# An order of its own for attention's first stage, with Pool's loads moved and routed rows scattered per token, in a two-layer AdaLN network on one core

## The reference, cut to what matters

```python
# x: 2 x 2048 x 256.  Layer 0
h = layernorm(x) * (1 + ca) + sa
Q, K, V = h @ W_q.T, h @ W_k.T, h @ W_v.T          # 16 heads of 16, rotary on Q and K
scores = Qr @ Kr.T / 4, causal;  pattern = softmax(scores)
x = x + ga * (pattern @ V) @ W_o.T
h = layernorm(x) * (1 + cb) + sb
x = x + gb * (h + h @ expert_w[argmax(h @ gate_w.T)].T)
# Layer 1
h = layernorm(x) * (1 + ca) + sa
x = x + ga * toeplitz_block(h)                      # u * T(v), with projections
h = layernorm(x) * (1 + cb) + sb
xn = h * rsqrt(mean(h * h) + eps) * ln_w
vals, idx = top_k(xn @ Wg + bg, 2);  topk_w = softmax(vals)
y_e = (silu(xn @ W1a[e] + b1a[e]) * (xn @ W1b[e] + b1b[e])) @ W2[e] + b2[e]     # F = 1024, 8 experts
x = x + gb * sum over the two chosen e of topk_w[e] * y_e
```

## Time and profile before

| what | value |
|---|---|
| median of 3 runs (lowest to highest) | 2665.64 us (2662.68 to 2666.26) |
| the profiled execution: its time / its span | 2663.03 us / 2661.1 us |
| mean granted clock of TensorE | 0.916 |
| busy: PE / DVE / ACT / Pool | 84% / 64% / 47% / 32% |
| DVE's 640 reduces of maxima (line 892) | 651.9 us, 1061 ns mean |
| Pool's 512 masks (line 705) | 143.3 us, 292 ns mean |
| zero fill of `y_slots` | 73 DMAs of 512 KB |
| first score product to the last of attention | about 301 to 1210 us |

### The profile page before, as it was taken

One profiled execution on the slowest core, in us unless ns is written; L12 is line 12 of the kernel. 1 busy time (PEld: TensorE's weight loads), 2 busy tenths in 40 slices (PEclk: granted clock), 3 DMA queues, 4 the chain that ended last, 5 costly groups with the idle time before them and its releaser, 6 DMA issues. The chain is left out here.

```text
span 2661.1 us, 39725 instructions
## 1 busy us (share of the span) xinstructions
PE 2231.8 (84%) x12968; PEld 1413.0 (53%) x12968; DVE 1693.0 (64%) x2599; ACT 1260.2 (47%) x2419; POOL 859.6 (32%) x1041
## 2 busy tenths in 40 slices
PE   3984898999989899996799699853999999999930
PEld 1762233333333333325577456553888888888830
DVE  4873877777777778844688768753545555545544
ACT  1331376766757677773223344412445555545520
POOL 2445302122121211110655413543223333323256
PEclk8996699999999999998899899966999999999975
DMA  4368604042140400002860100115444344434324
GB/s 164 107 144 166 91 2 65 5 62 35 33 65 3 64 3 3 2 1 67 351 256 0 31 1 17 40 44 182 136 152 141 133 149 141 146 121 133 123 76 126
DMA packets 138336, 238.26 MB, mean 90 GB/s; under 512 B 14768, under 2 KB 101552, under 8 KB 136752
## 3 DMA queue, kind: packets, MB, share of 16 engines
q1 hardware_dynamic: 122128, 181.44, 19.8%
q0 software_dynamic: 14928, 50.35, 10.7%
q10 hardware_dynamic: 1104, 4.20, 1.1%
HBM read 150.88 MB, written 85.07 MB: 89 GB/s over the span
## 5 line engine op out<-in xcount | busy, mean ns | idle before, releaser
L892 DVE TENSOR_REDUCE tile_max<-p_m 128x2 f32<-128x1024 f32 (+3 forms) x640 | 651.9, 1061 | 172.5 <-PE p_m L751 102.8
L854 ACT ACTIVATE probs<-p_s 128x512 f32<-128x512 f32 (+3 forms) x1280 | 596.3, 534 | 273.2 <-PE p_s L764 267.7
L2052 PE MATMUL p_up<-f_xT,f_w 128*128 128x512 f32 (+1 forms) x2304 | 468.9, 352 | 8.6 <-POOL f_w L2182 8.6
L2052 PEld LDWEIGHTS p_up<-f_xT,f_w 128*128 128x128 f32 x2304 | 372.2, 189 | 62.0 <-issue 8.9
L2182 POOL TENSOR_TENSOR f_w<-f_raw,f_w 128x1024 fp32r<-128x1024 f32 x96 | 230.9, 2409 | 504.0 <-ACT f_w L2104 504.0
L751 PE MATMUL p_m<-ka,qa 96*128 96x512 bf16 (+3 forms) x1280 | 363.3, 366 | 27.1 <-PEq L327 15.3
L705 POOL TENSOR_SCALAR_AFFINE_SELECT probs<-probs 128x128 f32<-128x128 f32 x512 | 143.3, 292 | 732.2 <-ACT probs L854 724.7
L764 PE MATMUL p_s<-qa,ka 99*128 99x512 bf16 (+3 forms) x1280 | 353.5, 353 | 11.5 <-ACT probs L854 6.9
L778 PE MATMUL p_o<-probs,va 128*32 128x512 f32 (+3 forms) x2560 | 305.9, 550 | 29.5 <-POOL probs L705 29.5
L2067 PE MATMUL p_y<-f_w,f_hidden 128*128 128x256 f32 x1872 | 261.8, 286 | 23.0 <-DVE f_y L2158 11.7
L2067 PEld LDWEIGHTS p_y<-f_w,f_hidden 128*128 128x128 f32 x1872 | 241.1, 188 | 45.4 <-issue 23.5
(11 more groups left out here) (242 smaller groups left out, 2602.3 us busy)
## 6 DMA issues: line engine op xcount, KB each, us to landing
y_slots<-zeros SPq DMA_DIRECT2D x73, 512.0 KB, 5.6
f_raw<-in_W1a SPq DMA_DIRECT2D x24, 1024.0 KB, 6.5
f_raw<-in_W1b SPq DMA_DIRECT2D x24, 1024.0 KB, 8.6
f_raw<-in_W SPq DMA_DIRECT2D x24, 1024.0 KB, 11.1
qk_scr<-parts SPq DMA_DIRECT2D x48, 256.0 KB, 2.3
qa<-qk_scr POOLq DMA_DIRECT2D x42, 256.0 KB, 15.6
ka<-qk_scr POOLq DMA_DIRECT2D x42, 256.0 KB, 17.4
v_scr<-wqkv_raw SPq DMA_DIRECT2D x32, 256.0 KB, 3.1
```

The lines of the kernel that those rows point to most:

```text
L854: nc.scalar.activation(probs[:, (buf * UNITS + n) % NPROBS, h, lo:CH], p_s[:, s_bank(("exp", HG * n + h), buf), lo:CH], ACT.Exp, scale=DH ...
L892: nc.vector.tensor_reduce(out=tile_max[:, 2 * hp:2 * hp + 2, i, bank], in_=p_m[:, at_bank, :, 0:width], op=ALU.max, axis=AX.X).then_inc(ma ...
L2052: last = nc.tensor.matmul(p_up[:, f % 2, ab, 0:size], w1[:, wh, ab * KT + kt, f * P:(f + 1) * P], xT[:, t % 2, xh, kt, 0:size], start=(kt, ...
```

## The change

1. *Projections*: the ones rows of ka0 are set by Pool right after `rstd`, ahead of the three subtractions. The first stage's loads go in three parts, after chunks 4, 5 and 6 (4, 4 and 5 DMAs), on ACT as before; ACT's loop over the chunks is unrolled.
2. *Attention*: stage 0 has a lead of 24 maxima (chunks 0 and 1) and a table of its own, three maxima a unit in the first 18. The other stages keep their table. The ones rows of ka1 and ka2 are set after unit 11's mask of stage 0, and the loads of stage s + 2 are issued after unit 11's mask of stage s (1 to 5), in place of those of stage s + 3 after the last mask of stage s.
3. *Top-1 experts*: no zeros, no zero fill.
4. *Layer 1*: rows get 258 columns, the last two the token's number and its first expert's number + 1. DVE waits for the routing tables before its first centring, copies the token numbers, and has one small operation more in each of the five choices and one at the end.
5. *Routed experts*: DVE finds for each slot the row of `y_rows` that it belongs to (token number, plus `SECOND` if it is the second choice, an own dump row if it is none), five small operations a tile, and SP waits for them before it loads the next rows. Pool scatters `f_y`, 78 indirect DMAs of 128 rows, a tile's after the last first-layer piece of the tile behind it. SP's 24 stores go.
6. *Combine*: SP loads both rows of all tokens in 16 plain DMAs of 512 KB, ACT does the first product, DVE the other three; Pool has nothing to do.

```diff
                 root(nc, pool, k, 0)
+                pool.wait_ge(k.rstd_ready, 1)
+                nc.gpsimd.memset(k.ka0[QROWS:QROWS + SPLIT, :, :], 1.0).then_inc(ones0_set, 1)
+                pool.wait_ge(ones0_set, 1)
                 for n, cols in enumerate(columns):
...
+                def load_first_stage(third):
+
+                    if third == 0:
+                        for qk in range(2):
+                            act.wait_ge(parts_stored[qk], 16 * SPLIT * CPS)
+                        act.wait_ge(va_stored, 16 * NHG * CPS)
+                    load_scores_rows(act, k, 0, k.qa0, k.ka0, k.stage0_loaded, range(2 * third, 2 * third + 2))
+                    if third == 2:
+                        load_values(act, k, 0, k.va0[:, :, :], k.stage0_loaded)
...
-                    if isinstance(i, int) and i == NCH - 2:
-                        load_first_stage()
                     if not last_chunk(i):
                         round_hT(i + 1, 1 - par)
                     take_v(i)
                     split(i, 0)
                     split(i, 1)
+                    if isinstance(i, int) and CPS <= i < CPS + 3:
+                        load_first_stage(i - CPS)
...
-        MAX_LEAD = 22
+        MAX_LEAD, FIRST_LEAD = 2 * 22, 24
...
+        FIRST_MAXIMA = [(2, 1)] * 18 + [(1, 1)] * 6 + [(2, 1), (1, 1)] * 2 + [(1, 1)] * 12
+        assert sum(map(sum, FIRST_MAXIMA)) == NMAX + MAX_LEAD - FIRST_LEAD
+        FIRST_TURN = {9: (2, False), 20: (3, False), 24: (0, True), 32: (1, True)}
...
-                for rows in ka:
-                    last = nc.gpsimd.memset(rows[QROWS:QROWS + SPLIT, :, :], 1.0)
-                last.then_inc(ones_set, 1)
                 for s in range(NS):
                     for n in diag_no:
                         mask(s, n)
-                    if s + NBUF < NS:
-                        load(s + NBUF)
+                        if diag_no[n] == 2 * TPC - 1:
+                            if s == 0:
+                                pool.wait_ge(diag_masked, 2 * TPC)
+                                for n1 in range(1, NBUF):
+                                    nc.gpsimd.memset(ka[n1][QROWS:QROWS + SPLIT, :, :], 1.0).then_inc(ones_set, 1)
+                                pool.wait_ge(ones_set, NBUF - 1)
+                            elif s + NBUF - 1 < NS:
+                                load(s + NBUF - 1)
 
...
                             pe.wait_ge(max_placed, 16 * (CPS * s + c + 1))
+                            if c == 0 and not first(s):
+                                pe.wait_ge(ones_set, NBUF - 1)
...
-                for u in range(2 * MAX_LEAD):
+                for u in range(FIRST_LEAD):
                     if u >= 2:
                         pe.wait_ge(max_taken, u - 1)
                     maximum(0, 0, u, u % 2)
                     if ends_chunk(u):
                         turn_maxima(max_units[u][0], max_units[u][0])
-                pe.wait_ge(ones_set, 1)
...
-                sp.wait_ge(zeros_set, 1)
-                with sp.Fori(0, NSLOT // ST) as t:
-                    sp.dma_start(k.y_slots[at(t, ST, ST), :].rearrange("(p u) d -> p (u d)", p=P), zeros[:, :]
-                                 ).then_inc(slots_zeroed, 16)
-                sp.wait_ge(slots_zeroed, 16 * (NSLOT // ST))
...
                 c_own.add(nc.vector.memset(cum[:, :, :], 0.0))
+                dve.wait_ge(route_loaded, 16 * ROUTE_LOADS)
+                c_own.add(nc.vector.tensor_copy(row_ids[:, :, 0], token_no))
                 dve.wait_ge(rstd_all, 1)
...
                         sp.wait_ge(turned, t)
+                        sp.wait_ge(y_to_ready, t)
...
-                def store(t):
-                    size = SIZES[t]
-                    row = sp.value_load(k.rows[0:1, t:t + 1], min_val=0, max_val=NSLOT - ST)
-                    sp.wait_ge(y_ready, t + 1)
-                    sp.dma_start(k.y_slots[bass.ds(row, size), :].rearrange("(u p) d -> p u d", p=P), y[:, 0:size // P, :]
-                                 ).then_inc(y_stored, 16)
-
...
+                def find_rows(t):
+
+                    blocks = SIZES[t] // P
+                    dve.wait_ge(x_loaded, 16 * t + 16)
+                    nc.vector.tensor_scalar(second[:, 0:blocks], x[:, 0:blocks, D + 1], k.owner_ids[:, t:t + 1], float(SECOND),
+                                            ALU.not_equal, ALU.mult).then_inc(second_ready, 1)
+                    nc.vector.scalar_tensor_tensor(out=dump[:, 0:blocks], in0=x[:, 0:blocks, D], scalar=0.0, in1=dump_no[:, 0:blocks],
+                                                   op0=ALU.is_equal, op1=ALU.mult).then_inc(second_ready, 1)
+                    dve.wait_ge(second_ready, 4 * t + 2)
+                    nc.vector.tensor_tensor(dump[:, 0:blocks], dump[:, 0:blocks], x[:, 0:blocks, D], ALU.add
+                                            ).then_inc(second_ready, 1)
+                    dve.wait_ge(second_ready, 4 * t + 3)
+                    nc.vector.tensor_tensor(second[:, 0:blocks], second[:, 0:blocks], dump[:, 0:blocks], ALU.add
+                                            ).then_inc(second_ready, 1)
+                    dve.wait_ge(second_ready, 4 * t + 4)
+                    if t >= 3:
+                        dve.wait_ge(y_stored, 16 * blocks_to[t - 2])
+                    nc.vector.tensor_copy(y_to[:, t % 3, 0:blocks], second[:, 0:blocks]).then_inc(y_to_ready, 1)
+
...
+                def scatter(t):
+                    pool.wait_ge(y_to_ready, t + 1)
+                    pool.wait_ge(y_ready, t + 1)
+                    for u in range(SIZES[t] // P):
+                        pool.indirect_dma_start(out=k.y_rows[:, :],
+                                                out_offset=bass.IndirectOffsetOnAxis(ap=y_to[:, t % 3, u:u + 1], axis=0),
+                                                in_=y[:, u, :], in_offset=None).then_inc(y_stored, 16)
+
                 for t in range(NTILES):
...
+                    if t:
+                        scatter(t - 1)
+                scatter(NTILES - 1)
+                pool.wait_ge(y_stored, 16 * blocks_to[NTILES])
...
-                        pool.wait_ge(done, i - 1)
-                    for u in range(TPC):
-                        for q in range(2):
-                            t = i * TPC + u
-                            pool.indirect_dma_start(out=ys[:, i % 2, q, u, :], out_offset=None, in_=k.y_slots[:, :],
-                                                    in_offset=bass.IndirectOffsetOnAxis(ap=k.slots[:, q, t:t + 1], axis=0),
-                                                    ).then_inc(gathered[i % 2], 16)
...
+                    for q in range(2):
+                        row = q * SECOND + 1 + i * CH
+                        sp.dma_start(ys[:, q, rows_of(i), :], k.y_rows[row:row + CH, :].rearrange("(u p) d -> p u d", p=P)
+                                     ).then_inc(loaded[i], 16)
+                for i in range(NCH):
...
+                for i in range(NCH):
+                    act.wait_ge(loaded[i], 16 * 2)
+                    for t in range(i * TPC, (i + 1) * TPC):
+                        nc.scalar.activation(res[:, t, :], ys[:, 0, t, :], ACT.Copy, scale=k.weights[:, 0, t:t + 1]
+                                             ).then_inc(weighed, 1)
 
```

240 lines of the change are left out of this document (124 added, 116 removed).

## The result

The changed kernel took **2594.78 us** in the median of four runs (2593.84 to 2603.96), against 2665.2 for the kernel before on the same chip: ratio 0.9745, interval 0.9722 to 0.9768. That is 70 us less where 90 were forecast. The time lies in the range (2555 to 2606), 19 above the forecast of 2576, and nearest to rival E's 2591.

The account below looks back on a forecast made before the run. PE, working 84% of the span, was taken to bound the kernel on average, with gains where it waits. Eight parts summed to −89.5 us from the profiled 2663.0, plus 2.6 for the median: 2576, range 2555 to 2606.

Parts of the forecast that it names:

- rival E: Attention: the moved loads make chunk 3's place late, three us in each of five stages, 2591 in all; chance 0.15.
- Part 2: End of projections: first-stage loads in thirds shorten ACT's wait, −8 us (−17 to −4).
- Part 7: Routed loop: Pool's 78 scatters fit into its idle time, DVE's small operations into DVE's; +2 us (0 to 15).
- Terms 1: Projections: ka0's ones-row memset on Pool ahead of the subtractions holds up DVE's first centring, +6.6 us (0 to 6.9).
- 6: Layer 1: DVE's first centring waits for all four routing tables, +5.2 us (0 to 6); small routing operations, +0.6.
- Part 8: Combine: plain loads replace gathers and DVE takes 4.3 us per chunk, −53 us (−56 to −40).
- Rivals C and D: C: routed scatters hold up the weights, 2871, chance 0.03. D: combine bound by DMA at 118 GB/s, 2639, chance 0.04.
- Part 3: Attention stage 0: the shorter lead wins 10 us at the start and gives it back inside the stage, +1 (−11 to +6).
- 109.5 from unit 4: Stage 0: 14 units bound by DVE at 3.5 us, the other 22 at 2.75; 109.5 us against 99 now.
- Rival B: Attention: small row-maxima places pass Pool's load backlog, so the stage gains 11 us instead of losing 1; 2564, chance 0.15.
- Part 4: Attention: Pool's loads moved to mid-stage remove the issues' delay and chunk 2's 9.4 us place wait, −43 us (−43 to −25).
- it just fits: Attention with moved loads: chunk 3's place is through at about +62 us of a stage, before PE needs it at +64.

Follow-up runs that it names:

- fourth run: The kernel before with only the changed projections and attention; zero fill, layer 1, routed loop and combine as before: 2643.72 us, ratio 0.9934.
- tenth: The changed kernel with ka0's memset behind the weight subtractions, token numbers copied after layer 1's first centrings, and a DVE probe of the last scatters' landing: 2583.05 us.
- The last run: The ninth run's kernel with the change's own stage 0 order (lead 24), Pool's first loads given out between the places: 2565.26 us, ratio 0.9628.
- ninth run: The changed kernel with lead 44, Pool's loads behind chunk 1's place but clear of the loop's jump, memset and token copy later, a DVE probe: 2552.65 us.

## Why the prediction was right or wrong

**Direction and range** held. That the sum fell inside the range is partly luck: attention gained 36.6 us less than forecast and parts 2 and 7 gave 16.6 more. Terms 1 (+6.6, measured +6.6), 6 (5.0 of the 5.2 us for the late table; 12 us came back when memset and copy were moved) and, within 7 us, 8 held. Term 1 held by its mechanism: the first centring lasts 7.09 us beside the memset where it took 0.41 before. Term 5 (−0.9) is too small to be seen: from the last place to the first centring are 356.8 us with the fill in the fourth run and 356.9 without it in the tenth. Rivals C and D fell: a scatter took 0.96 us on Pool, PE never waited for a piece in the loop but once at its start, as before, and in the combine DVE waited only ahead of its first operation.

**Part 3 failed, and is the largest error.** It said +1 (−11 to +6). The trace of after gives +17, outside its bounds: from the first maximum to chunk 2's place in stage 1 before takes 191.4 us, less 8.1 for the load in it, 183.3; after takes 200.7. Undoing the order gave back 21, since the old order also loses the 5.7 us operation of the earlier trace rows now that the memsets are gone. The head of the part was right: chunk 1 placed at 58 us behind the first maximum (302 − 244), measured 58.5 (291.79 − 233.29). The step that failed is "109.5 from unit 4", which was to cost 10.5 us against before. From unit 4 to chunk 2's place in stage 1, before took 123.7 us including a load's 8.1, so 126.1 was expected; after took 142.2. The working had 14 units of three maxima from unit 4 on where the table has 16, which is 1.5 us. The rest is of another kind. I had priced the units by averages, DVE's 3.5 us or PE's 2.75, at full clock. They begin at half clock after a wait of ten microseconds (0.50, then 0.86 and 0.83; what is missing from full clock in these three windows is 8.1 us, an upper bound of its price), and then neither engine is saturated: each waits for the other in turn, so a unit takes longer than either average. The last run shows that this second half remains, 6 to 8.7 us, with free places. How much of it is the table of the order and how much the shared time with Pool was not separated.

**Rival B fell.** By the Trainium skill ("DMA: Bandwidth & Descriptors", Queues, rings and completion order) each DMA engine takes turns between queue rows, packet by packet, from which I had estimated that the small place passes the backlog. Places took 4.9 to 13.9 us behind a load's backlog and mostly 1.4 without one, so if the engines do take turns, it doesn't carry a transfer of this size through in two or three microseconds.

**Part 4 failed by its size**, −43 for a measured −27.6. Its first step named two causes for the 43.4 us; only the issues are one (29.2 us of waits), while the place of 9.4 us held nobody up. Of the rest, 14.2 us, the loop's jump has 3.1, and PE's other waits are 0.4 us at most. But TensorE's granted clock is 0.97 over a period with a load and 1.00 over the one of 108.17, and 0.71 in the 10 us around the first of these waits. That is up to 3.5 us a period (an estimate, 0.03 of 116), enough for the rest. And "it just fits" was wrong by little: the load of chunk 3's place is issued 7.5 to 8.7 us behind its store, and PE waited 7.5 us for such places in five stages, at most 2.1 at once. The clock falls behind some of them (0.66 and 1.00 in the two windows of 10 us after the wait in stage 1). Rival E named this mechanism with 3 us per stage. The excess of the five loaded periods of after over 108.2 is 20.6 us, 4.1 per stage. One of them, 116.6, carries the jump of the loop too. It was 3 us above its neighbours before also, and I took it into the 43.4 as if a load had made it. The ninth run brought the others to 108 to 109.5 but that one only to 114.7.

**Part 2** was undersized: −8 for −15.9 in the trace and −19.8 in the run that undid it. The step that failed is the last third's delay of 9 us; the split waited 7.62, 3.0 more than the 4.63 of an undisturbed chunk.

**Part 7** had the wrong sign: +2 for −6.7. The scatters did fit. PE's products of the loop, before and after (busy us, mean ns, idle before):

```profile
L2052 PE MATMUL p_up<-f_xT,f_w 128*128 128x512 f32 (+1 forms) x2304 | 468.9, 352 | 8.6 <-POOL f_w L2182 8.6
L2067 PE MATMUL p_y<-f_w,f_hidden 128*128 128x256 f32 x1872 | 261.8, 286 | 23.0 <-DVE f_y L2158 11.7 <-DVE f_hidden L2150 8.6
```
```profile
L2078 PE MATMUL p_up<-f_xT,f_w 128*128 128x512 f32 (+1 forms) x2304 | 462.5, 350 | 8.9 <-POOL f_w L2241 8.9
L2093 PE MATMUL p_y<-f_w,f_hidden 128*128 128x256 f32 x1872 | 256.0, 283 | 28.8 <-DVE f_hidden L2195 15.0 <-DVE f_y L2203 12.6
```

Both kinds are some 6 us shorter in sum, for the same instructions, and the waits ahead of the second grew by 5.8. With before's loop behind after's attention they took 468.7 and 261.8 again. Several things differ between the loops: SP's stores, Pool's scatters, DVE's small operations and the two columns more; which of them shortens a matmul was not tried.

**Part 8** was −46.4 in place of −53. DVE's 4.1 us per chunk was better than the 4.3 forecast. (Before, DVE's waits for a chunk's gathers came to 47.4 us over seven chunks, up to 15.1, and not 5.24 each.) The error is in "16 plain loads follow": the first of them comes 11.3 us behind the start of the last scatter's issue, and the landing is 3.2 of these. The other 8.1 have no named cause. With Pool as the engine that issues the loads the gap is 0.8 us shorter. Nothing else was tried, and the cause stays open.

**What adds up.** The old lead gives 21, the small mends 12, together 33 of the 42 us of the ninth run. The other 9 are, by difference, the loads behind chunk 1's place with the jump kept free of them.

## What to carry to other kernels

A shorter lead gives back what it took unless the engine that makes the leading work has room later: count both engines per unit, and count the waits and the half clock between them, not their averages. When a bulk load is moved away from one small transfer, list which small transfer is next, and also the program's jumps: here instructions come through the same DMA engines. A wait in a profile is worth its own length only if its waiter was the last; the place of 9.4 us cost little, and Pool's 5.7 us of issuing cost all of itself.
